# An adaLN transformer block for 32 batches: the set-up of the first batches reordered, and the first batch's stacks loaded in six parts

## The chip, the cores and the metric

The kernel runs on one core of a Trainium2 chip. The core has a matrix engine (TensorE), an engine for elementwise work and reductions (VectorE), one for activation functions (ScalarE), a general one (GpSimd), and a queue engine (SyncE, SP) that here only issues transfers. Each works through its own list of instructions in order and waits on semaphores for the others. The metric is the device time of one execution in microseconds.

## The reference, cut to what matters

```python
# x: (32, 256, 128); 16 heads of 8 channels; feed-forward width 352
mod = (silu(c) @ wmod).reshape(32, 6, 1, 128)
sa, ca, ga, sb, cb, gb = (mod[:, i] for i in range(6))
ga = (2 * (ga >= 0) - 1) * maximum(abs(ga), 0.25)        # gb in the same way
h = layernorm(x) * (1 + ca) + sa
# attention over channels-by-time, heads split along the flattened (t, d) axis
q, k, v = ((h @ W + b).reshape(32, 16, 8, 256) for W, b in ((Wq, bq), (Wk, bk), (Wv, bv)))
attn = softmax(einsum('bhdt,bhds->bhts', k, v) * temperature)
x = x + ga * einsum('bhdt,bhts->bhds', q, attn).reshape(32, 256, 128)
h = layernorm(x) * (1 + cb) + sb
# fp4_linear: both operands rounded blockwise (16) to the FP4 grid
x = x + gb * fp4_linear(silu(fp4_linear(h, w_gate)) * fp4_linear(h, w_up), w_down)
```

## The kernel before

One batch of 256 x 128 values is the unit of work, and 32 of them pass through a software pipeline written out by hand. Each engine has a function `step(k)`, called for k = 0 to 38 and followed by a list of its own for the end of the kernel. In `step(k)` the line `at(k, lag, task)` does `task` for batch `k - lag` if there is such a batch; a line `if k == n: task()` places work that is done once. The order of the lines in `step` is the order of that engine's instructions, so moving a line moves the work in the queue. What is in the queue behind a wait waits too.

A batch goes this way. SP loads x into `x_in` (`load_first_x` for batch 0). VectorE takes the statistics (`stats1_rows`, `variance1`, which also makes the negated mean), GpSimd the reciprocal root (`rstd1_pow`) and the normalised rows (`normalise1`). TensorE transposes them (`x_transpose`), ScalarE copies the result out with shift and scale (`h_out`). TensorE projects keys and values into one bank (`kv_proj`) and queries into another (`q_proj`). The float32 keys and values are split into a high and a low part by four VectorE instructions (`v_hi`, `k_hi`, `v_lo`, `k_lo`), eight DMAs store the parts to an internal DRAM tensor (`store_k_hi` and so on, semaphore `split_stored`), and five DMAs load them back in another arrangement: `v_stack` (512 KB) and four row groups of `k_stack` (128 KB each), all on one semaphore, `stack_loaded`. `k_stack` must be zeroed first, in four pieces per buffer (`zero_k(p, i)` on GpSimd); each of the two buffers is zeroed once.

`scores(b, c, j)` for j = 0 to 15 then makes one head's scores, two matmuls each, in the order `head(j) = j % 4 * 4 + j // 4`; head h needs group h // 4 of `v_stack`, and row group h % 4 of `k_stack`. VectorE takes the row maxima of two heads at a time (`maxes`), ScalarE the exponentials (`exps`), TensorE the product with the queries (`mix`). The second half of the block (gates, second norm, quantised feed-forward) follows some steps later.

Set-up work is placed among the first steps. TensorE's `condition()` multiplies the shift and scale part of the modulation, VectorE's `shift_and_scale()` copies it out; `h_out(0)` needs it. TensorE's `gates()` and VectorE's `gates()` (six instructions) make the other four parts, which SP stores (`store_mod`) and loads per batch (`load_mod`). The feed-forward weights are quantised once, in a chain that goes back and forth between VectorE (`ff_max`, `ff_recip`, `ff_exponent`, `ff_magic`) and GpSimd (`ff_scale`, `ff_y`, `ff_add`, `ff_sub`, `ff_rescale`). The three bias rows and the temperatures come with SP's `load_set_up`; ScalarE's and VectorE's `biases()` split the biases.

In the kernel before, `scores(0, c, 0)` waits for all five loads at once, and `kv_proj(0)` for the biases ahead of its first matmul.

## Time and profile before

| | |
|---|---|
| median of 3 runs | 618.02 us (617.03 to 620.19) |
| the profiled execution: its own time | 614.91 us |
| its span, from the first to the last instruction | 613.1 us |
| mean granted TensorE clock over the span | 0.969 |
| busy: TensorE, VectorE, ScalarE, GpSimd | 555.5, 567.7, 555.8, 507.3 us |

Times in the trace count from the start of the span. "Busy" sums the time in which an engine works on instructions; a wait stands as idle time ahead of an instruction, with the engine or transfer that ended it. An issue of a DMA and the landing of its data are different things: the landing time is counted from the start of the issue. The granted clock is 1.00 where TensorE is granted 2.4 GHz, and 0.50 where it is granted 1.2 GHz.

### The profile page before, as it was taken

To read this page: it belongs to the slowest core of one execution; us is meant where nothing else is said; L and a number is where in the kernel's file an instruction comes from. 1 tells how busy PE (TensorE), PEld (TensorE's weight loads), DVE (VectorE), ACT (ScalarE), POOL (GpSimd) and SP (SyncE) were. 2 spreads that over 40 slices of the span, in tenths; PEclk is the share of its full clock that TensorE was granted. 3 is DMA by queue.
4 is the path that set the end of the run, shared out by engine and by line. 5 is a ranking of instruction groups with operands and counts; after the bars stand their busy time and mean duration, and the time that the engine had idled before them with its cause. 6 is when DMAs were issued, how large, how long until landed. Compare 5 with 4: busy or idle time off the path is not lost.

```text
span 613.1 us, 15512 instructions
## 1 busy us (share of the span) xinstructions
PE 555.5 (91%) x4336; PEld 383.2 (63%) x4336; DVE 567.7 (93%) x1124; ACT 555.8 (91%) x2281; POOL 507.3 (83%) x710
## 2 busy tenths in 40 slices
PE   4478899999999999999999999999999999998865
PEld 2355555666666666666666666666666666666554
DVE  3478799999999999999999999999999999999996
ACT  2199899999999999999999999999999999999721
POOL 7343478899999999999999999999999999998751
PEclk9669799999999999999999999999999999999987
DMA  3746654555555655565455665556555666543000
GB/s 92 199 123 157 163 150 129 156 158 150 148 149 149 170 150 148 153 173 162 136 151 148 164 171 154 155 143 166 144 145 149 158 174 165 151 128 95 10 10 26
DMA packets 87872, 86.12 MB, mean 140 GB/s; under 512 B 8550, under 2 KB 83532, under 8 KB 87788
## 3 DMA queue, kind: packets, MB, share of 16 engines
q1 hardware_dynamic: 85628, 83.37, 50.5%
q10 hardware_dynamic: 2160, 1.77, 1.1%
q8 instruction: 36, 0.59, 0.4%
q14 instruction: 48, 0.39, 0.3%
HBM read 47.29 MB, written 37.81 MB: 139 GB/s over the span
## 4 chain that ended last, share of the span: by engine, by line
ACT 54%; PE 16%; issue 12%; DVE 12%; POOL 2%; DMA 2%; SPq 1%; DVEq 0%; ACTq 0%; POOLq 0%
ACT probs L785 48%; DVE neg_max L961 6%; PE score_ps L1453 5%; PE bank L1531 5%; PE bank L1520 3%; ACT hT L795 2%; DVE silu_g L1079 2%; ACT hid_T L819 2%; ACT q_T L801 1%; DVE h_mag L931 1%; PE bank L1556 1%; DMA k_stack<-split_dram 1%; PE bank L1498 1%; POOL hid_q L345 1%; ACT tanh_g L813 1%
## 5 line engine op out<-in xcount | busy, mean ns | idle before, releaser
L785 ACT ACTIVATE probs<-score_ps,neg_max 128x256 f32<-128x256 f32 x1024 | 483.6, 553 | 5.2 <-DVE neg_max L961 4.2
L961 DVE TENSOR_REDUCE neg_max<-score_ps 128x4 f32<-128x1024 f32 x256 | 312.0, 1219 | 18.5 <-PE score_ps L1453 15.8
L785 ACT ACTIVATION_READ_ACCUMULATOR probs<-score_ps,neg_max 128x1 f32 x1024 | 292.8, 286 | 0.0
L1453 PE MATMUL score_ps<-v_stack,k_stack 128*128 128x256 f32 x1024 | 233.6, 331 | 25.6 <-ACT probs L785 22.7
L1453 PEld LDWEIGHTS score_ps<-v_stack,k_stack 128*128 128x128 f32 x1024 | 154.9, 193 | 109.6 <-ACT probs L785 89.9
L1498 PE MATMUL bank<-probs,q_z 128*32 128x256 f32 x2048 | 131.5, 387 | 0.0
L1498 PEld LDWEIGHTS bank<-probs,q_z 128*32 128x32 f32 x2048 | 57.3, 110 | 41.7 <-issue 2.1
L1556 PEld LDWEIGHTS bank<-wd_T,hid_T 118*128 118x128 f32 x384 | 52.6, 201 | 7.5 <-ACT hid_T L819 1.3
L1556 PE MATMUL bank<-wd_T,hid_T 118*128 118x128 f32 x384 | 55.6, 285 | 0.5 <-ACT hid_T L819 0.5
L1520 PE MATMUL bank<-wgu_T,h_T 128*128 128x352 f32 x128 | 51.5, 484 | 1.7 <-ACT h_T L808 0.5
L345 POOL TENSOR_TENSOR hid_q<-hid_r,hid_sc 128x704 f32<-128x704 bf16 x31 | 43.0, 1386 | 6.4 <-DVE hid_r L340 6.3
L1531 PE MATMUL bank<-wgu_T,h_T 128*128 128x352 f32 x128 | 48.0, 459 | 0.0
L336 POOL TENSOR_TENSOR hid_q<-hid_q,hid_mag 128x704 f32<-128x704 f32 x30 | 45.8, 1527 | 1.8 <-DVE hid_mag L935 1.8
L819 ACT ACTIVATE hid_T<-bank 118x384 f32<-118x384 f32 x64 | 33.3, 523 | 14.2 <-PE bank L1545 14.0
L1473 PE MATMUL bank<-w_kv,hT 128*128 128x256 f32 x128 | 42.0, 422 | 1.4 <-ACT hT L795 1.4
L813 ACT ACTIVATE tanh_g<-bank 128x352 f32<-128x352 f32 x64 | 39.0, 609 | 4.6 <-PE bank L1520 4.5
L340 POOL TENSOR_TENSOR hid_r<-hid_q,hid_mag 128x704 bf16<-128x704 f32 x28 | 42.8, 1530 | 0.0
L318 POOL TENSOR_TENSOR hid_q<-hid,hid_rs 128x704 f32<-128x704 f32 x30 | 41.6, 1388 | 0.6 <-DVE hid_rs L1098 0.2
L516 POOL TENSOR_TENSOR rstd<-var,minus_half 128x2 f32<-128x2 f32 x32 | 22.8, 712 | 20.7 <-DVE var L969 18.2
L530 POOL TENSOR_TENSOR rstd<-var,minus_half 128x2 f32<-128x2 f32 x32 | 30.2, 945 | 11.7 <-DVE nm L972 7.9
L1545 PE MATMUL bank<-ident,hid_q 128*118 128x128 f32 x192 | 28.8, 286 | 10.9 <-POOL hid_q L345 6.5
L268 POOL TENSOR_SCALAR h_c<-x,nm,rstd 128x128 f32<-128x128 f32 x62 | 31.8, 520 | 3.2
(119 smaller groups left out, 877.8 us busy)
## 6 DMA issues: line engine op xcount, KB each, us to landing
v_stack<-split_dram SPq DMA_DIRECT2D x32, 512.0 KB, 4.2
split_dram<-kv_hi SPq DMA_DIRECT2D x124, 128.0 KB, 2.6
split_dram<-kv_lo SPq DMA_DIRECT2D x124, 128.0 KB, 2.7
k_stack<-split_dram SPq DMA_DIRECT2D x124, 128.0 KB, 4.5
mod_bc<-mod_dram SPq DMA_DIRECT2D x32, 256.0 KB, 3.9
x_in<-in_L_attn_x_dram SPq DMA_DIRECT2D x32, 128.0 KB, 3.2
out_dram<-out_t SPq DMA_DIRECT2D x32, 128.0 KB, 3.6
split_dram<-kv_hi ACTq DMA_DIRECT2D x4, 128.0 KB, 2.4
```

The costliest lines, as they stand in the source:

```text
L336: ve.tensor_tensor(hid_q[:, :], hid_q[:, :], hid_mag[:, :], ALU.add).then_inc(hid_t_made, 1)
L340: ve.tensor_tensor(hid_r[:, :], hid_q[:, :], hid_mag[:, :], ALU.subtract)\
L345: ve.tensor_tensor(blocks16(hid_q[:, :]), blocks16(hid_r[:, :]), spread16(hid_sc[:, :]), ALU.mult).then_inc(hid_dq_made, 1)
L785: nc.scalar.activation(probs[p][:, h, a, :], score_ps[:, j % 4, a, :], ACT.Exp, bias=neg_max[:, p, n:n + 1], accum_out=row_sum[:, p, h, a: ...
L813: nc.scalar.activation(tanh_g[:, a, :], bank_gate[a][:, 0:FF], ACT.Tanh, scale=0.5)\
L819: nc.scalar.activation(hid_T[:, a, :, :], bank_hidT[a][0:HN, 0:HT * 128].rearrange("p (t n) -> p t n", n=128), ACT.Copy)\
L961: nc.vector.tensor_reduce(neg_max[:, p, 4 * u:4 * u + 4], score_ps[:, lo:lo + 2, :, :].rearrange("p b a n -> p (b a) n"), AX.X, ALU.max, n ...
L1453: done = nc.tensor.matmul(score_ps[:, j % 4, a, :], k_stack[p][:, h, 128 * a:128 * a + 128], v_stack[p][:, h // R, :], start=True, stop=True)
L1498: done = nc.tensor.matmul(bank_mix[32 * g:32 * g + 32, 0:T], q_z[p][:, a, g, r, :], probs[p][:, R * g + r, a, :], start=(i == 0), stop=(i ...
L1520: nc.tensor.matmul(bank_gate[a][:, 0:FF], h2_T[:, 128 * a:128 * a + 128], wgu_T[:, 0, :], start=True, stop=True).then_inc(gate_ps_made[a], 1)
L1531: nc.tensor.matmul(bank_up[a][:, 0:FF], h2_T[:, 128 * a:128 * a + 128], wgu_T[:, 1, :], start=True, stop=True).then_inc(up_ps_made[a], 1)
L1556: done = nc.tensor.matmul(bank_down[:, a * D:(a + 1) * D], hid_T[:, a, t, :], wd_T[:, t, :], start=(t == 0), stop=(t == HT - 1))
```

## The change

Six things are done. The order of the set-up work on all engines is another: SP issues `w_mod`, then biases and temperatures, and only then the feed-forward weights; `condition()` is TensorE's first step; VectorE takes batch 0's statistics ahead of `shift_and_scale`, `biases` and the weight maxima; GpSimd zeroes only one piece of `k_stack` ahead of batch 0's rstd, three behind its `normalise1`, and the four of the second buffer behind batch 1's. `gates()` goes behind `q_proj(0)` on TensorE and behind `variance1(1)` on VectorE, ahead of `ff_max(0)`. Batch 0's stacks are loaded in six parts, each with a semaphore of its own: four row groups of `k_stack` and two halves of `v_stack`; SP issues k 0, v 0, k 2, and ScalarE v 1, k 1, k 3, ahead of `h_out(1)`. Batch 0's scores wait at j = 0 for v 0 and k 0, at j = 2 for v 1, at j = 4, 8 and 12 for k 1, 2 and 3. `kv_proj(0)` waits for the biases behind its first matmul. Batches from 1 on are loaded as before.

```diff
@@ helpers
+        def wait_stacks(eng, b):
+            if b == 0:
+                for part in (*first_v, *first_k):
+                    eng.wait_ge(part, 16)
+            elif b > 0:
+                eng.wait_ge(stack_loaded[b % 2], (b + 1) // 2 * LOADS * 16)
...
+        def load_first_v(eng, i):
+            wait_dma(eng, split_stored, 0, STORES * 16)
+            groups = slice(i * G // 2, (i + 1) * G // 2)
+            eng.dma_start(v_stack[0][:, groups, :].bitcast(F32),
+                          split_dram[0, 1, groups].rearrange("g r s j n -> (r s j) g n")).then_inc(first_v[i], 16)
+
+        def load_first_k(eng, r):
+            eng.wait_ge(k_zeroed[0], G)
+            wait_dma(eng, split_stored, 0, STORES * 16)
+            eng.dma_start(k_stack[0][32 * r:32 * r + 32, r:H:R, :].bitcast(F32),
+                          split_dram[0, 0, :, r].rearrange("g s j n -> (s j) g n")).then_inc(first_k[r], 16)
@@ SP, step
+                if k == 0:
+                    load_first_x()
+                if k == 0:
+                    load_w_mod()
+                if k == 0:
+                    load_set_up()
                 if k == 2:
                     load_ff(1)
-                if k == 0:
-                    load_first_x()
...
+                if k == 5:
+                    load_first_stacks()
+                if k == 5:
+                    load_first_ks()
                 at(k, 5, load_stacks_first)
-                if k == 3:
-                    load_set_up()
                 at(k, 3, load_x)
                 at(k, 5, store_v_hi)
-                if k == 0:
-                    load_w_mod()
                 if k == 5:
                     store_mod()
@@ GpSimd, step
+                if k == 0:
+                    zero_q()
+                if k == 0:
+                    zero_k(0, 0)
...
                 at(k, 6, normalise1)
+                if k == 7:
+                    ff_y(1)
                 if k == 7:
                     ff_y(2)
...
                 if k == 7:
-                    zero_k(1, 3)
+                    ff_y(0)
                 if k == 6:
-                    zero_k(1, 2)
+                    zero_k(0, 1)
                 if k == 6:
                     zero_k(0, 2)
                 if k == 6:
                     zero_k(0, 3)
+                if k == 6:
+                    ff_scale(2)
+                if k == 6:
+                    ff_scale(1)
                 if k == 7:
+                    zero_k(1, 0)
+                if k == 7:
+                    zero_k(1, 1)
+                if k == 7:
+                    zero_k(1, 2)
+                if k == 7:
+                    zero_k(1, 3)
@@ ScalarE, step
+                if k == 6:
+                    load_first_va()
+                if k == 6:
+                    load_first_ka()
                 at(k, 6, load_k_stack)
...
+                if k == 5:
+                    biases()
                 at(k, 5, h_out)
@@ VectorE, step
-                if k == 7:
-                    gates()
                 at(k, 7, v_hi)
...
-                if k == 4:
-                    shift_and_scale()
...
                 at(k, 6, stats1_rows)
-                if k == 2:
-                    ff_max(2)
...
                 at(k, 6, variance1)
+                if k == 7:
+                    gates()
+                if k == 7:
+                    ff_max(0)
+                if k == 7:
+                    ff_exponent(1)
+                if k == 7:
+                    ff_recip(0)
+                if k == 6:
+                    shift_and_scale()
+                if k == 6:
+                    biases()
+                if k == 6:
+                    ff_max(2)
+                if k == 6:
+                    ff_max(1)
+                if k == 6:
+                    ff_recip(2)
                 if k == 6:
                     ff_recip(1)
@@ TensorE, scores
-                if j == 0:
-                    wait_dma(pe, stack_loaded, b, LOADS * 16)
-                    if b == 0:
+                if b == 0:
+                    if j == 0:
                         pe.wait_ge(modT_made, 2)
                         pe.wait_ge(mod_step, 6)
+                    if j % (G // 2) == 0 and j < G:
+                        pe.wait_ge(first_v[j // (G // 2)], 16)
+                    if j % G == 0:
+                        pe.wait_ge(first_k[j // G], 16)
+                elif j == 0:
+                    wait_stacks(pe, b)
@@ TensorE, kv_proj
-                    pe.wait_ge(bias_step, 3)
-                    pe.wait_ge(pad_zeroed, 2)
                 for a in range(2):
...
+                    if b == 0:
+                        pe.wait_ge(bias_step, 3)
+                        pe.wait_ge(pad_zeroed, 2)
                     done = nc.tensor.matmul(cols, ones_r[:, 0:128], b_pad[:, D:3 * D], start=False, stop=True,
@@ TensorE, step
+                if k == 0:
+                    condition()
...
                 at(k, 7, q_proj)
+                if k == 7:
+                    gates()
...
-                if k == 4:
-                    gates()
-                if k == 3:
-                    condition()
```

## Rows read from the trace of the kernel before

**Rows 1.** Busy time by stretches: stretch, its length, busy us (instructions) of each engine, granted clock, DMA share, GB/s.

```profile
30.00:84.00 54.00, 44.42 (x281) 29.06 (x285) 42.23 (x72) 50.89 (x215) 24.80 (x42) 0.84 0.57 146
84.00:534.00 450.00, 434.50 (x3541) 300.84 (x3541) 443.54 (x865) 449.07 (x1861) 414.93 (x574) 1.00 0.57 154
```

**Rows 2.** The chain of waits, 0 to 60 us: start, us, what.

```profile
9.33 0.73 POOL rstd L516
...
11.15 0.70 PE bank L1461 x2
...
12.54 1.19 PE bank L1473 x2
...
14.80 0.23 PE bank L1476
...
17.80 3.23 DMA split_dram<-kv_lo
...
22.10 5.40 DMA k_stack<-split_dram
```

**Rows 3.** The timeline of TensorE: start, us, instruction, [idle before and what ended it].

```profile
6.55 1.92 PE L1419 MATMUL score_ps<-w_mod,silu_c 128*32 128x512 f32 x2
...
15.30 0.52 PE L1486 MATMUL bank<-ones_r,b_pad 128*128 128x256 f32 x1
...
25.29 0.78 PE L1476 MATMUL bank<-b_pad,ones_r 128*128 128x256 f32 x1
...
27.54 1.88 PE L1453 MATMUL score_ps<-v_stack,k_stack 128*128 128x256 f32 x8 [0.41 <-DMA k_stack<-split_dram]
...
57.30 0.67 PE L1473 MATMUL bank<-w_kv,hT 128*128 128x256 f32 x2
```

**Rows 4.** The timeline of SP's queue: start and us of DMA issues.

```profile
1.18 0.40 SPq L389 DMA_DIRECT2D x_in<-in_L_attn_x_dram  x1
...
2.58 1.38 SPq L413 DMA_DIRECT2D w_ff<-in_L_ffn_w_up_dram  x3
...
5.77 0.61 SPq L405 DMA_DIRECT2D temp<-_L_attn_temperature_dram  x1
```

**Rows 5.** DMA issues, 1.1 to 2.9 us: count, KB each, us to landing.

```profile
x_in<-in_L_attn_x_dram SPq DMA_DIRECT2D x1, 128.0 KB, 2.9
...
w_ff<-in_L_ffn_w_up_dram SPq DMA_DIRECT2D x1, 64.0 KB, 3.3
```

**Rows 6.** The timeline of VectorE.

```profile
7.82 0.42 DVE L977 BATCH_NORM_STATS2 stats<-x_in 128x6 f32<-128x256 f32 x1
...
9.32 0.41 DVE L911 TENSOR_SCALAR mod_rows<-score_ps 32x256 f32<-32x256 f32 x1
...
10.81 0.55 DVE L921 SCALAR_TENSOR_TENSOR mod_rows<-mod_rows,mod_tmp 32x256 f32<-32x256 f32 x1
...
17.10 0.54 DVE L926 TENSOR_REDUCE w_am<-w_ff 128x24 f32<-128x384 f32 x1
```

**Rows 7.** The timeline of GpSimd.

```profile
3.80 1.84 POOL L505 MEMSET k_stack<- 128x1024 f32 x2
...
17.73 0.31 POOL L261 TENSOR_SCALAR w_sc<-w_am 128x24 f32<-128x24 f32 x1 [3.96 <-DVE w_am L926]
...
30.87 0.91 POOL L617 TENSOR_TENSOR w_ff<-w_ff,w_mag 128x384 f32<-128x384 f32 x1 [7.92 <-DVE w_mag L935]
```

**Rows 8.** The timeline of ScalarE.

```profile
6.89 1.07 ACT L750 ACTIVATE b_pad<-b_raw 1x384 fp32r<-1x384 f32 x2 [3.17 <-DMA b_raw<-in_L_attn_bv_dram]
...
30.06 0.47 ACT L785 ACTIVATE probs<-score_ps,neg_max 128x256 f32<-128x256 f32 x1 [0.56 <-DVE neg_max L961]
...
70.88 0.47 ACT L785 ACTIVATE probs<-score_ps,neg_max 128x256 f32<-128x256 f32 x1 [1.59 <-DVE neg_max L961]
```

**Rows 9.** Busy time by stretches, with the columns of the first group.

```profile
43.00:62.50 19.50, 15.18 (x125) 10.09 (x124) 16.59 (x27) 18.56 (x80) 6.86 (x12) 1.00 0.56 143
64.00:69.50 5.50, 5.38 (x32) 2.92 (x32) 2.93 (x7) 5.03 (x21) 3.18 (x7) 0.50 0.56 165
```

More of the change, by code:

```diff
@@ L131, in adaln_block @@
         stack_loaded = [sem(f"stack_loaded{i}") for i in range(2)]
+        first_v, first_k = ([sem(f"first_{n}{i}") for i in range(m)] for n, m in (("v", 2), ("k", R)))
         out_stored = [sem(f"out_stored{i}") for i in range(2)]
@@ L223, in store_k_hi_on @@
         def store_k_hi_on(eng, b, c):
-            wait_dma(eng, stack_loaded, b - 2, LOADS * 16)
+            wait_stacks(eng, b - 2)
             wait_batches(eng, k_hi_made, b + 1)
@@ L228, in store_v_hi_on @@
         def store_v_hi_on(eng, b, c):
-            wait_dma(eng, stack_loaded, b - 2, LOADS * 16)
+            wait_stacks(eng, b - 2)
             wait_batches(eng, v_hi_made, b + 1)
@@ L246, in load_v_stack_on @@
                 .then_inc(stack_loaded[c % 2], 16)
+        def load_first_v(eng, i):
[8 more added lines that the diff above has]
+                          split_dram[0, 0, :, r].rearrange("g s j n -> (s j) g n")).then_inc(first_k[r], 16)
         def load_k_stack_on(eng, b, c, r):
[L249 removed]
+            if b == 1:
                 eng.wait_ge(k_zeroed[b], G)
@@ L439, in store_v_lo, with load_first_stacks, load_first_ks @@
                     store_v_lo_on(sp, b, c)
+            def load_first_stacks():
+                load_first_k(sp, 0)
+                load_first_v(sp, 0)
+            def load_first_ks():
+                load_first_k(sp, 2)
             def load_stacks_first(b, c):
-                if b < 2:
+                if b == 1:
                     load_v_stack_on(sp, b, c)
@@ L637, in step @@
                 at(k, 10, scale2)
-                if k == 3:
-                    zero_k(0, 0)
                 at(k, 10, shift2)
@@ L642, in step @@
                 at(k, 10, h2_scale)
-                if k == 0:
-                    zero_q()
                 if k == 11:
                     ff_sub(2)
-                if k == 7:
-                    ff_y(1)
                 at(k, 9, q_scaled)
@@ L654, in step @@
                 at(k, 12, hid_rescale)
+                if k == 9:
+                    ff_add(2)
+                at(k, 10, h2_sub)
+                at(k, 6, normalise1)
+                if k == 7:
+                    ff_y(1)
                 if k == 7:
                     ff_y(2)
-                if k == 9:
-                    ff_add(2)
-                if k == 1:
-                    zero_k(1, 0)
-                if k == 3:
-                    ff_scale(1)
                 if k == 7:
-                    zero_k(1, 3)
-                at(k, 10, h2_sub)
-                at(k, 6, normalise1)
+                    ff_y(0)
                 if k == 6:
-                    zero_k(1, 2)
+                    zero_k(0, 1)
                 if k == 6:
@@ L672, in step @@
                     zero_k(0, 3)
+                if k == 6:
+                    ff_scale(2)
+                if k == 6:
+                    ff_scale(1)
                 if k == 7:
-                    ff_y(0)
+                    zero_k(1, 0)
[5 more added lines that the diff above has]
+                    zero_k(1, 3)
                 if k == 11:
@@ L679, in step @@
                 at(k, 9, residual1)
-                if k == 1:
-                    zero_k(1, 1)
                 at(k, 10, h2_rescale)
@@ L692, in step @@
                     ff_sub(1)
-                if k == 3:
-                    zero_k(0, 1)
                 at(k, 11, hid_y)
-                if k == 2:
-                    ff_scale(2)
             for k in range(TAIL):
@@ L770, in store_v_lo, with load_first_va, load_first_ka @@
                     store_v_lo_on(act, b, c)
+            def load_first_va():
+                load_first_v(act, 1)
+                load_first_k(act, 1)
+            def load_first_ka():
+                load_first_k(act, 3)
             def load_k_stack(b, c):
-                if b < 2:
+                if b == 1:
                     for r in range(R // 2, R):
@@ L834, in step @@
                 at(k, 7, exps, 0)
-                if k == 4:
-                    biases()
                 at(k, 7, exps, 1)
@@ L1259, in step @@
                 at(k, 6, variance1)
+                if k == 7:
[16 more added lines that the diff above has]
+                    ff_recip(2)
                 if k == 6:
                     ff_recip(1)
-                if k == 6:
-                    biases()
                 at(k, 10, h2_magic)
-                if k == 7:
-                    ff_max(0)
-                if k == 2:
-                    ff_recip(2)
                 at(k, 11, silu, 1)
-                if k == 2:
-                    ff_max(1)
-                if k == 7:
-                    ff_exponent(1)
                 if k == 8:
```

7 lines of the change are left out of this document (removed).

## The prediction

> **What bounds the kernel now.** I read the busy time by stretches first [rows 1]. From 84 to 534 us ScalarE works 449.07 of 450 us: the exponentials of all batches follow one another without a hole, and this stretch can only be moved, not shortened, by a change to the ramp. From 30 to 84 us ScalarE already works 50.89 of 54 us, so 3.11 us of idle time stand there. Ahead of 30.06 us, where the first exponential starts [rows 8], there is none at all. The kernel's ramp is thus what the change can move: the question is when `exps(0, 0)` starts, and whether the 3.11 us behind it grow.
>
> The chain of waits [rows 2] shows what sets 30.06. Batch 0's rstd starts on GpSimd at 9.33, its transpose on TensorE at 11.15, `kv_proj(0)` at 12.54, with its banks full at 14.80 + 0.23 = 15.03. The split stores end at 17.80 + 3.23 = 21.03, and the stack loads at 22.10 + 5.40 = 27.50. Then scores, maxima, exponentials. A second chain of nearly the same length runs beside it: `kv_proj(1)`, `q_proj(1)` stand ahead of `scores(0, 0)` in TensorE's order, and the score row shows TensorE idle only 0.41 us ahead of it [rows 3]. The loads were late by 0.41 us, no more; without them the scores would start at 27.13.
>
> **The change, batch 0.** Before, rstd(0) at 9.33 stood behind weight scales and memsets on GpSimd. `x_in(0)` was issued at 1.18 and took 2.9 us, so it lay there at 4.1 [rows 4, 5]; the statistics take 0.42 us on VectorE [rows 6] and the reduction behind them about 0.2 by my estimate, hence 4.8. After the change GpSimd has only `zero_q` and one `zero_k` ahead; two of these start at 3.80 and take 1.84 us, 0.92 each [rows 7], so GpSimd is free at 4.72. From rstd to the start of the transpose the chain took 11.15 − 9.33 = 1.82, so the transpose can start at 4.8 + 1.82 = 6.6. TensorE must do `condition()` first; that ended where `gates()` began, at 6.55, held by `w_mod` [rows 3], which keeps its place in SP's order. I take 6.65 for the transpose. Transpose to full banks took 15.03 − 11.15 = 3.88, hence 10.53: batch 0 comes **4.50 us** earlier.
>
> Three things stand beside this. The set-up DMAs (three bias rows and the temperatures) took 5.77 + 0.61 − 3.96 = 2.42 us to issue, 0.6 each [rows 4]; they now begin two issues of 0.46 behind 1.18, at 2.1, so the third bias row goes out at 3.3. With the 2.9 us of `x_in` to landing it is there at 6.2, with the 3.3 of `w_up` at 6.6 [rows 5]; ScalarE's two copies take 1.07 us [rows 8] and stand ahead of `h_out(0)`, whose transpose ends at 7.35. So they end at 7.3 or 7.7: I take 0, and 0.4 late as the bound. `w_down` and `w_up` move back by those 2.4 us: `w_up`, last issued at 3.5 and now at 5.9, with 3.3 us to landing is there at about 9, its maximum ends at 9.5, and GpSimd scales it behind three `zero_k` that end at 6.6 + 2.8 = 9.4. VectorE's reciprocals, which now stand ahead of `v_hi(0)`, end near 10.5, just as the banks fill: 0 by my sum, 0.5 late as the bound. The wait for the biases moves behind the first projection matmul: that gives up to that matmul's 0.6 us if they are late, and nothing where they are in time.
>
> **The change, batch 1.** Before, its banks were full at 25.29 + 0.78 = 26.07, which is 11.04 after those of batch 0 [rows 3]. Now `gates()` stands ahead of its transpose on TensorE, and on VectorE ahead of `ff_max(0)`, whose scale on GpSimd stands ahead of rstd(1). Counted from batch 0's full banks: `q_proj(0)` ends at 15.30 + 0.52 − 15.03 = 0.79; `gates()` takes 1.92 (two matmuls), to 2.71; its six VectorE steps took 11.36 − 9.32 = 2.04, to 4.75 [rows 6]; `ff_max(0)` and the hand-over took 17.73 − 17.10 = 0.63, to 5.4; the scale 0.31 [rows 7] with a hand-over of the same size as the others, under 0.1, to 5.79; rstd to transpose 1.82 and transpose to full banks 3.88, to 11.5. That is **0.45 us worse** than 11.04: `gates()` costs 2.71 + 2.04 here, and what was there before in its place, two scalings `ff_y` and one memset between rstd's neighbours, has moved behind `normalise1(1)`. Bounds: with TensorE at its upper level `gates()` would take half, and the chain would gain up to 0.65.
>
> ScalarE passes three load issues ahead of `h_out(1)` and waits for the stores first. The stores landed 21.03 − 15.03 = 6.0 after the banks [rows 2]; two issues took 22.10 − 21.03 = 1.07, so three bring it to 7.6, and the transpose of batch 1 ends at 11.5 − 3.88 + 0.7 = 8.3: covered by 0.7. On SP, `store_mod` and `load_mod(0)` keep their places behind the loads, and the gates are ready at 4.75, ahead of them; batch 0 needs them only behind its mix, which follows all its exponentials.
>
> **The parts.** The loads took 27.5 − 21.03 = 6.47 from the stores' landing to the last landing. Undivided they would land at 6.0 + 6.5 = 12.5 after the banks; the scores can start at 11.5 + 1.06 (27.13 − 26.07) = 12.56. So the 0.41 us wait goes even without the parts, and waiting for them singly gives 0 to 0.4. The shorter first part could save more only if TensorE had nothing ahead of the scores, and it has `kv_proj(1)`.
>
> Behind the scores nothing of the order is new: 27.54 to 30.06 is 2.52 us, and ScalarE sat idle 0.56 us ahead of its first exponential [rows 8], so its own queue (the stores of `kv_lo(1)`, `q_T`) has that much slack, of which the missing 0.41 us wait uses most. The four `zero_k(1, ·)` move behind `normalise1(1)`: 3.7 us on GpSimd, which then stood idle for 7.92 us before `ff_add(1)` [rows 7]; with the 0.8 us scalings ahead they end 5 us before batch 1's stores have landed, which the loads wait for as well.
>
> **Sum:** 4.50 − 0.45 + 0.41 = 4.46, say 4.5 us. First exponentials at 25.6. ScalarE is full behind them, so all is carried to the end. The profiled execution took 614.91 us (span 613.1 and 1.8 around it), which would become 610.4. It lies 3.1 below the shown median of 618.02; the shift against the median gives **613.5**.
>
> **Rivals.** 0.5% of this kernel is 3.1 us, about what a measurement can tell from no change.
>
> A, the sum as above: 613.5, own range 612 to 615. Chance 0.48.
>
> B, half of it lost in new waits: biases late 0.4, reciprocals ahead of `v_hi(0)` 0.5, and one more TensorE stall of the kind that left ScalarE idle 1.59 us at 70.88 [rows 8]. That stall stands in a stretch where the granted clock was 0.50 (1.2 GHz) and TensorE worked 5.38 of 5.5 us [rows 9]. One such stall alone: 4.5 − 1.6 = 2.9, 615.1; with the 0.5 ahead of `v_hi(0)`: 615.6. For it: the margins in the ramp are tenths of a microsecond. Chance 0.24.
>
> C, nothing gained: the ramp is shorter but batch 1's part, stores of `kv_lo(1)`, loads, four more memsets, holds ScalarE's queue at `load_k_stack(1)`. It needs those to slip by 4.5; the memsets have 5 us of slack, the stores move with the banks. 618. Chance 0.07.
>
> D, more than the sum: `kv_proj(1)` at the upper level. Two of its matmuls take 1.19 us in the ramp and 0.67 once the granted clock is 1.00 in the stretch around them [rows 2, 3, 9], so it would end 1.1 earlier, and `gates()` gives 0.65: 6.2, 611.8. If the 3.11 us of idle time [rows 1] vanish too, 608.7. TensorE is now busy without a hole from `kv_proj(0)` through `gates()`, which speaks for it; a hole of 6 us follows, which speaks against. Chance 0.15.
> The Trainium skill (TensorE: Matmul & The Clock Gate, Part 1) says that the point at which the clock rises varies from run to run of the same kernel. By that rule `kv_proj(1)` and `gates()` can come out on either level in different runs, and a median over runs lies between A and D. The changes of level in this trace agree in so far as they follow neither batch nor stage; one trace can't show the variation.
>
> E, slower: the upper level's stretch is lost. From 43 to 62.5 us TensorE worked 15.18 of 19.5 us at 1.00 [rows 9]. At half that clock the same work takes 30.4 us, 10.9 more than there is; less the 4.5, the kernel is 6.4 slower, 624.4. Each microsecond at the lower level costs 0.56, so 7.6 us of loss, which makes it slower by over 0.5%, needs 13.6 us of that stretch. Against it: after 64 to 69.5, with TensorE full, the level rose again. Chance 0.06.
>
> **Numbers.** Faster by over 0.5% in A and D: 0.63; within in B and C: 0.31; slower 0.06. The range leaves out the lower part of D, half of C and all of E: 610.0 to 618.5.
>
> **What would show it.** In the profile after: rstd(0) at 4.8, `kv_proj(0)`'s banks full near 10.5, `gates()` right behind `q_proj(0)`, rstd(1) near 16.3, `kv_proj(1)`'s banks near 22, first scores near 23.1 with no wait for a load ahead of them, first exponentials near 25.6, ScalarE idle 3 us in the 54 us behind. Wrong if a DMA ends the wait ahead of the scores, if `gated` or the stores hold VectorE, or if the idle time behind the first exponentials is over 5 us.

## The result, and the profile after

| | before | changed |
|---|---|---|
| median on the same chip | 617.52 us (6 runs, 616.79 to 620.46) | 613.49 us (6 runs, 611.20 to 614.23) |
| ratio | | 0.9931, 95% interval 0.9913 to 0.9949 |
| profiled execution: own time, span | 614.91, 613.1 us | 614.23, 611.3 us |

The changed kernel is 4.0 us faster in the medians, 0.7%. Its profiled span is only 1.8 us shorter. That difference is explained below; the span of one execution is not the effect.

The timeline of TensorE after, which answers to [rows 3]:

```profile
5.32 1.04 PE L1458 MATMUL score_ps<-silu_c,w_mod 128*128 128x32 f32 x4 [2.44 <-DMA w_mod<-in_L_wmod_dram]
6.48 0.69 PE L1510 MATMUL bank<-ident,xn 128*128 128x128 f32 x2
7.87 1.19 PE L1520 MATMUL bank<-w_kv,hT 128*128 128x256 f32 x2 [0.70 <-ACT hT L835]
...
9.57 0.78 PE L1526 MATMUL bank<-b_pad,ones_r 128*128 128x256 f32 x1
...
11.34 1.42 PE L1463 MATMUL score_ps<-w_mod,silu_c 128*32 128x512 f32 x2
17.39 0.69 PE L1510 MATMUL bank<-ident,xn 128*128 128x128 f32 x2 [4.63 <-POOL xn L556]
18.78 1.19 PE L1520 MATMUL bank<-w_kv,hT 128*128 128x256 f32 x2 [0.70 <-ACT hT L835]
...
20.47 0.78 PE L1526 MATMUL bank<-b_pad,ones_r 128*128 128x256 f32 x1
...
22.11 1.22 PE L1502 MATMUL score_ps<-v_stack,k_stack 128*128 128x256 f32 x8
25.75 3.44 PE L1502 MATMUL score_ps<-v_stack,k_stack 128*128 128x256 f32 x8 [2.41 <-ACT probs L825]
```

The reader is to see three things. Batch 0's banks are full at 9.57 + 0.78 = 10.35, where [rows 2] had 15.03. Then comes a hole of 4.63 us ahead of batch 1's transpose, ended by GpSimd. And the first score row, at 22.11, has no wait ahead of it at all; the one in [rows 3] waited 0.41 us for a load.

The granted clock that the profile gives is 1.00 over these first microseconds, but that is no reading. The first entry in the trace's list of clock changes is a rise, at 12.1 us here and at 15.4 in the profile of before, and ahead of the first entry the profile gives 1.00. The durations up to there are those of the lower level (the pair at 7.87 took 1.19 us).

The timelines of GpSimd, of ScalarE and of VectorE after:

```profile
4.72 0.72 POOL L549 TENSOR_TENSOR rstd<-var,minus_half 128x2 f32<-128x2 f32 x1
...
15.24 0.30 POOL L283 TENSOR_SCALAR w_sc<-w_am 128x24 f32<-128x24 f32 x1 [5.36 <-DVE w_am L970]
15.62 0.72 POOL L549 TENSOR_TENSOR rstd<-var,minus_half 128x2 f32<-128x2 f32 x1
```

```profile
16.03 0.43 ACTq L261 DMA_DIRECT2D v_stack<-split_dram  x1
16.55 0.91 ACTq L267 DMA_DIRECT2D k_stack<-split_dram  x2
18.11 0.56 ACT L835 ACTIVATE hT<-bank,mod_T 128x256 f32<-128x256 f32 x1 [4.27 <-PE bank L1510]
...
24.31 0.38 ACT L841 ACTIVATE q_T<-bank 128x256 f32<-128x256 f32 x1 [5.63 <-issue]
24.59 0.47 ACT L825 ACTIVATE probs<-score_ps,neg_max 128x256 f32<-128x256 f32 x1
```

```profile
22.90 1.23 DVE L1005 TENSOR_REDUCE neg_max<-score_ps 128x4 f32<-128x1024 f32 x1
```

GpSimd is held 5.36 us by VectorE's maximum of the gate weights, which stands behind `gates()`; that is the wait that the change put ahead of batch 1's rstd. The first exponential follows `q_T` without a hole, and the maxima that it needs were done at 22.90 + 1.23 = 24.13, 0.46 us earlier: it is now ScalarE's own queue (four issues of stores for batch 1, then `q_T`) that holds it, not the maxima as in [rows 8]. From batch 1's full banks to the first exponential it is 24.59 − 21.25 = 3.34 us.

**Where the time went after that.** All exponentials run on ScalarE in order, so the execution can be cut at the start of the first exponential of batches 0, 3 and 31 (the 1st, 97th and 993rd of 1024 in ScalarE's timeline). I did this for every profile of this study. "Low" is how long the granted clock was 0.50 between the first two cuts, from stretches of half a microsecond.

| kernel | first exponential | to batch 3 | low in it | batch 3 to 31 | from there to the end of the span |
|---|---|---|---|---|---|
| before | 30.06 | 51.23 | 17 | 480.45 | 51.4 |
| before, second profile (`b_again`) | 29.77 | 51.11 | 17 | 480.47 | 54.5 |
| changed | 24.59 | 53.02 | 23.5 | 480.48 | 53.2 |
| changed, second (`a_again`) | 25.07 | 52.01 | 20.5 | 480.49 | 53.0 |
| changed, third (`a_again2`) | 24.49 | 52.91 | 23.5 | 480.43 | 53.3 |
| `b_parts` | 29.29 | 51.97 | 20.5 | 480.49 | 53.1 |
| `a_whole` | 25.85 | 51.93 | 20.5 | 480.46 | 53.1 |
| `a_gates_old` | 26.03 | 52.85 | 24 | 480.47 | 53.3 |
| `a_gates_late` | 24.47 | 50.78 | 17 | 480.52 | 53.0 |
| `a_gates_hout` | 23.61 | 51.83 | 20.5 | 480.47 | 53.3 |
| `a_gates_hout_whole` | 25.33 | 51.94 | 23.5 | 480.45 | 51.3 |
| `a_fill` | 24.60 | 50.21 | 10 | 480.52 | 53.0 |
| `a_fill_mid` | 24.28 | 51.03 | 13.5 | 480.51 | 53.1 |
| `a_best` | 24.13 | 50.80 | 12 | 481.41 | 53.4 |

The gain at the first exponential was 5.5 us in the first pair of profiles. 1.8 of it was lost before batch 3, nothing in the 480 us behind, and 1.8 in the last part, where the first profile of before was lucky: the same kernel took 51.4 and 54.5 there. The clock goes with that too: in this last part it was at 0.50 for 10.6 us in the two profiles that took 51.3 to 51.4, for 13.7 to 15.6 in the ten that took 53.0 to 53.3, and for 17.2 in the one that took 54.5; `a_best` (10.2 us low, 53.4) is the exception. Over the profiles of the two kernels (two of before, three of the changed one), the change gains 5.2 us at the first exponential, loses 1.5 up to batch 3 and about 0.3 in the last part, in the mean.

The busy time by stretches of the changed kernel, with TensorE alone (stretch, its length, busy us, granted clock, DMA share, GB/s):

```profile
26.00:39.00 13.00, 11.67 (x35) 0.50 0.46 131
39.50:42.50 3.00, 1.85 (x12) 1.00 0.59 156
43.00:46.00 3.00, 3.00 (x19) 0.50 0.73 183
47.00:59.00 12.00, 9.71 (x77) 1.00 0.51 132
60.50:66.00 5.50, 5.39 (x40) 0.50 0.55 153
```

Against [rows 9], where the clock was 1.00 from 43 to 62.5 without a break, there is a further stretch at 0.50 near 43 to 46, when the first `mix` runs (from 44.7).

### The profile page after: what moved, and what is told of

Read it like the earlier page. It is cut to its first block, busy times and chain, and to the rows that moved or that the text cites. A ratio compares the mean times of both kernels' runs of the same rounds, so it can differ in the third digit from the quotient of the medians.

```text
span 611.3 us, 15522 instructions
## 1 busy us (share of the span) xinstructions
PE 558.3 (91%) x4336; PEld 385.6 (63%) x4336; DVE 568.7 (93%) x1124; ACT 555.9 (91%) x2281; POOL 507.3 (83%) x710
## 4 chain that ended last, share of the span: by engine, by line
ACT 52%; PE 18%; issue 13%; DVE 12%; POOL 3%; ACTq 1%; DVEq 0%; POOLq 0%
ACT probs L825 47%; DVE neg_max L1005 6%; PE score_ps L1502 6%; PE bank L1581 5%; PE bank L1570 3%; ACT hT L835 2%; DVE silu_g L1123 2%; ACT hid_T L859 2%; PE bank L1548 2%; PE bank L1606 1%; ACT q_T L841 1%; DVE h_mag L975 1%; POOL hid_q L367 1%; PE bank L1520 1%; DVE h_mag L979 1%
## 5 line engine op out<-in xcount | busy, mean ns | idle before, releaser
L1502 PE MATMUL score_ps<-v_stack,k_stack 128*128 128x256 f32 x1024 | 234.9, 333 | 24.2 <-ACT probs L825 21.7
L859 ACT ACTIVATE hid_T<-bank 118x384 f32<-118x384 f32 x64 | 33.3, 523 | 13.7 <-PE bank L1595 13.5
L1595 PE MATMUL bank<-ident,hid_q 128*118 128x128 f32 x192 | 28.5, 284 | 12.2 <-POOL hid_q L367 6.3
```

Source lines behind the costliest of these rows:

```text
L859: nc.scalar.activation(hid_T[:, a, :, :], bank_hidT[a][0:HN, 0:HT * 128].rearrange("p (t n) -> p t n", n=128), ACT.Copy)\
L1502: done = nc.tensor.matmul(score_ps[:, j % 4, a, :], k_stack[p][:, h, 128 * a:128 * a + 128], v_stack[p][:, h // R, :], start=True, stop=True)
```

## The experiments

Each kernel was timed beside the kernel before, in four groups, each on one chip: `a_again`, `a_whole`, `b_parts` and `a_gates_old`; `a_gates_late`, the two `a_gates_hout` and `a_fill`; `a_again2`, `a_fill_mid` and `a_best`; `b_again`. Apart from the kernel before (two profiles) and the changed one (three), each has one profile, so what is said of times within it rests on one execution. The first pair, above, is a group of its own.

**1. The changed kernel again (`a_again`), and once more (`a_again2`).** No edit.

> The changed kernel unchanged, for its spread and for a second profile. Theory S (the sum of the ramp): the first exponential starts at 24.6 us again, give or take 0.2, since everything ahead of it is set by instructions of fixed length. Theory C (the clock ate part of the gain): in the first profile the batches' exponentials started 5.5 us earlier at batch 0 but 3.7 us earlier from batch 3 on; if the TensorE clock's low stretches did that, the second profile shows low stretches at other places and another shift from batch 3 on, anywhere from 2.5 to 6. Rival (the order of work behind the ramp did it): the loss between batch 0 and batch 3 is again 1.8, to within 0.2. Time about 613.5.

> The changed kernel once more, on the chip of the two below, as their measure, and as a fourth profile of its clock. Both theories: ratio to the kernel before 0.991 to 0.993; from the first exponential to the start of batch 3's it takes 52 to 53 us, as in the two profiles so far.

Measured: 612.18 us, ratio 0.9915 (0.9894 to 0.9936), and 613.00 us, ratio 0.9924 (0.9896 to 0.9953). Three measurements of the same change thus give 0.9915 to 0.9931. The first exponential came at 25.07 and 24.49. The 0.6 us between them has one place: `gates()` took 1.92 us on TensorE in the one and 1.29 in the other, and everything behind it moves along. The timeline of TensorE of `a_again`:

```profile
11.34 1.92 PE L1463 MATMUL score_ps<-w_mod,silu_c 128*32 128x512 f32 x2
17.88 0.69 PE L1510 MATMUL bank<-ident,xn 128*128 128x128 f32 x2 [4.63 <-POOL xn L556]
```

The wait behind is 4.63 in all three profiles, and the transpose starts at 17.88 against 17.39 and 17.26. So theory S missed with 24.6 give or take 0.2: an instruction ahead of the first exponential is not of fixed length when the clock changes under it. The loss up to batch 3 was 0.8 instead of the rival's 1.8, with 3 us less at the low level. So theory C's variation exists, but the loss was not erratic: each of the three profiles shows 52.0 to 53.0, above the 51.1 and 51.2 of the kernel before. My range of 2.5 to 6 for the shift held (4.2 and 3.9), but it was too wide to be much of a test.

**2. The parts undone (`a_whole`).**

```diff
-                load_first_k(sp, 0)
-                load_first_v(sp, 0)
+                load_v_stack_on(sp, 0, 0)
+                load_k_stack_on(sp, 0, 0, 0)
...
-                    if j % (G // 2) == 0 and j < G:
-                        pe.wait_ge(first_v[j // (G // 2)], 16)
-                    if j % G == 0:
-                        pe.wait_ge(first_k[j // G], 16)
+                        wait_stacks(pe, 0)
```

> The changed order, but batch 0's stacks loaded as before: five DMAs on one semaphore, all awaited at the first score. Theory S: the scores stand behind the second batch's projections, so the loads (issued from 16.1, all landed by about 22.5) are late by at most 0.4 us, and ScalarE's own queue hides most of it: first exponential at 24.6 to 24.9, time within 0.3 us of the changed kernel. Rival P (the parts carry the gain): first exponential 1.5 us or more later, time 1.5 to 4 us longer.

Measured: 611.59 us, ratio 0.9917 (0.9897 to 0.9937), against `a_again`'s 0.9915 on the same chip. The timeline of TensorE shows why nothing is lost:

```profile
5.99 1.04 PE L1453 MATMUL score_ps<-silu_c,w_mod 128*128 128x32 f32 x4 [3.23 <-DMA w_mod<-in_L_wmod_dram]
7.25 0.69 PE L1502 MATMUL bank<-ident,xn 128*128 128x128 f32 x2 [0.22 <-POOL xn L552]
...
23.37 1.49 PE L1494 MATMUL score_ps<-v_stack,k_stack 128*128 128x256 f32 x8
```

The scores follow the projections without a wait, though all five loads were awaited at once. The first exponential was 0.78 later than in `a_again` (I expected at most 0.3 later), but by the rows that is the 0.77 by which the first transpose came late (7.25 against 6.48), waiting for GpSimd; the arrival of the first transfers varies, as `w_mod`'s does here. ScalarE's queue hides a late load as well: the first exponential came 3.34 us behind batch 1's full banks, as with the parts. The rival P falls: in this kernel the parts carry nothing.

**3. The parts alone (`b_parts`).** The order of before, the six loads and single waits of the change.

> The kernel before with the six parts and their single waits alone, order untouched. Theory S: only the 0.41 us wait ahead of the first score can go; first exponential at 29.6 to 30.06, time 0 to 0.4 us shorter than before. Rival P: first exponential 1.5 us or more earlier, time 2 to 4 us shorter than before.

Measured: 615.72 us, ratio 0.9986 (0.9971 to 1.0001), that is −0.9 us with an interval from −1.8 to +0.1. The timeline of TensorE:

```profile
26.24 0.78 PE L1520 MATMUL bank<-ones_r,b_pad 128*128 128x256 f32 x1
26.81 1.48 PE L1487 MATMUL score_ps<-v_stack,k_stack 128*128 128x256 f32 x8
```

The 0.41 us wait of [rows 3] is gone. The first exponential came at 29.29, 0.5 to 0.8 earlier than in the two profiles of before and outside the 29.6 to 30.06 expected. Against the first profile, 0.12 of the 0.77 is batch 1, whose banks were full that much earlier. The rest stands behind the banks: from them to the first exponential it was 3.99 us there (3.88 in `b_again`), with ScalarE waiting for maxima, and 3.34 here, with no such wait, exactly as in the changed kernel. The wait for the load had thus cost 0.5 to 0.65 us there, more than the 0.41 and 0.30 that TensorE stood idle; ScalarE's own queue sets the limit to what removing it can give. The rival's 2 to 4 us are excluded.

**4. Both `gates()` back in their old places (`a_gates_old`).** `gates()` in TensorE's step 4 and ahead of `v_hi(0)` on VectorE.

> The changed kernel with both gates() back where they stood: on TensorE ahead of batch 0's transpose, on VectorE ahead of v_hi(0). Theory S: batch 0's transpose comes 1.8 later (8.3), its banks are full at 12.1; batch 1 no longer waits for gates on VectorE, but ScalarE issues the loads only when the stores have landed, at 17.8, so h_out(1) goes at 19.3 instead of 18.1: first exponential at 25.8, 1.2 us later than in the changed kernel, time 1.2 longer. By the prediction's narrower view, in which the gates on VectorE cost batch 1 2.7 us and nothing else holds it, the first exponential would come no later than 24.6.

Measured: 611.58 us, ratio 0.9931 (0.9906 to 0.9956), which doesn't part it from `a_again`. The trace does: first exponential at 26.03 instead of 24.5 to 25.1, and the wait stands where it was expected, ahead of `h_out(1)` on ScalarE, which had been issuing loads:

```profile
19.54 0.56 ACT L835 ACTIVATE hT<-bank,mod_T 128x256 f32<-128x256 f32 x1 [3.87 <-issue]
```

Moving `gates()` behind the projections is worth 1.0 to 1.5 us at the first exponential, as batch 0's transpose no longer stands behind it. The narrower view, in which it could only cost, falls. But the 1.2 us of time that were expected did not show: the median is 0.6 below `a_again`'s. The single executions tell why. Three had a mean granted clock of 0.962 to 0.966 and took 613.1 to 615.5 us, four had 0.977 and took 610.6 to 611.6: one and the same kernel differs by more than the edit is worth, and the clock goes with it. All eighteen executions of the changed kernel have 0.962 to 0.969.

**5. VectorE's `gates()` behind `ff_max(0)` (`a_gates_late`).**

```diff
                 at(k, 6, variance1)
-                if k == 7:
-                    gates()
                 if k == 7:
                     ff_max(0)
+                if k == 7:
+                    gates()
```

> The changed kernel with VectorE's gates() behind ff_max(0) instead of ahead of it, so that batch 1's rstd on GpSimd no longer waits for the gates. Theory S: rstd(1) starts at 13.6 instead of 15.6 and the transpose of batch 1 ends at 16.0; but h_out(1) on ScalarE stands behind three load issues that wait for the stores (landed at 16.0, issued to 17.5), so of the 2 us only 0.6 reach kv_proj(1): first exponential at 24.0 to 24.4, time 0.6 us shorter than the changed kernel. Rival (the gates' wait alone held batch 1): first exponential 2 us earlier, at 22.6.

Measured: 612.88 us, ratio 0.9941 (0.9923 to 0.9959). Batch 1's rstd started at 13.44 instead of 15.62. ScalarE and TensorE:

```profile
16.38 0.42 ACTq L261 DMA_DIRECT2D v_stack<-split_dram  x1
16.90 0.91 ACTq L267 DMA_DIRECT2D k_stack<-split_dram  x2
17.93 0.56 ACT L835 ACTIVATE hT<-bank,mod_T 128x256 f32<-128x256 f32 x1 [4.10 <-issue]
```

```profile
15.44 0.69 PE L1510 MATMUL bank<-ident,xn 128*128 128x128 f32 x2 [3.01 <-POOL xn L556]
18.60 1.19 PE L1520 MATMUL bank<-w_kv,hT 128*128 128x256 f32 x2 [2.47 <-ACT hT L835]
...
22.45 1.19 PE L1502 MATMUL score_ps<-v_stack,k_stack 128*128 128x256 f32 x8 [0.45 <-DMA v_stack<-split_dram]
```

Of 2.2 us won at rstd, 0.2 reached `h_out(1)`: the transpose is done at 16.1, and ScalarE is still issuing loads until 17.8. The wait moved, and a second one (0.45 for `v_stack`) came up behind it. The first exponential at 24.47 is no earlier than in the best profile of the changed kernel. The expectation's mechanism was right, but its 0.6 us of gain was not seen, and the first exponential missed its 24.0 to 24.4.

**6. And ScalarE's three issues behind `h_out(1)` (`a_gates_hout`); the same with whole loads (`a_gates_hout_whole`).**

```diff
-                if k == 6:
-                    load_first_va()
-                if k == 6:
-                    load_first_ka()
                 at(k, 6, load_k_stack)
...
                 at(k, 5, h_out)
+                if k == 6:
+                    load_first_va()
+                if k == 6:
+                    load_first_ka()
```

> As a_gates_late, and ScalarE's three load issues behind h_out(1) instead of ahead of it. Theory S: h_out(1) goes at 16.1, kv_proj(1)'s banks are full at 19.3 instead of 21.25, the scores are then ready to start at 20.1, and only now do the loads come last: with the parts the first ones have landed at about 20.9. First exponential at 22.6 to 23.2, time 1.5 to 2 us shorter than the changed kernel. Rival (the parts never matter, the loads land together at 22.3): first exponential at 24.2 or later.

> As a_gates_hout, with batch 0's stacks loaded whole and awaited at once, as before the change. Theory S: the scores wait for the last load at 22.3 to 22.6, first exponential at 24.2 to 24.6: 1.5 us later than with the parts, which were worth nothing in the changed kernel. Rival (all transfers share the same engines and land together): no later than with the parts, to within 0.3.

Measured: 611.14 us, 0.9916 (0.9898 to 0.9934), and 612.12 us, 0.9934 (0.9915 to 0.9952), on the same chip. TensorE with the parts, then without:

```profile
18.82 0.78 PE L1536 MATMUL bank<-ones_r,b_pad 128*128 128x256 f32 x1
21.60 1.19 PE L1502 MATMUL score_ps<-v_stack,k_stack 128*128 128x256 f32 x8 [2.00 <-DMA v_stack<-split_dram]
```

```profile
19.59 0.78 PE L1528 MATMUL bank<-ones_r,b_pad 128*128 128x256 f32 x1
22.84 2.05 PE L1494 MATMUL score_ps<-v_stack,k_stack 128*128 128x256 f32 x8 [2.47 <-DMA k_stack<-split_dram]
```

Now the loads come last, and the parts count: scores start at 21.60 with them and at 22.84 without, the first exponential at 23.61 and 25.33. Both are later than the 22.6 to 23.2 and 24.2 to 24.6 expected. Of the 1.7 us between them, 1.2 is the loads; the rest is that the first row of scores took 1.19 us with the parts and 2.05 without, where the granted clock was 0.50. The parts count for less than they could, because of which part is late. The issues of the version with parts:

```profile
v_stack<-split_dram ACTq DMA_DIRECT2D x1, 256.0 KB, 3.6
k_stack<-split_dram SPq DMA_DIRECT2D x2, 128.0 KB, 4.0
v_stack<-split_dram SPq DMA_DIRECT2D x1, 256.0 KB, 4.9
```

The half that the first score needs is SP's, issued second in its queue at 16.43, and takes 4.9 us; ScalarE's half, needed two heads later, was issued at 15.97 and takes 3.6. Another order of the two was not tried. In time the two intervals overlap; that the parts give 1.0 us there is the trace's word and the medians' direction, not a settled ratio.

**7. TensorE kept busy (`a_fill`, `a_fill_mid`).** The second leaves out the 16 ahead of `x_transpose`.

```diff
+            def fill(n):
+                for _ in range(n):
+                    nc.tensor.matmul(bank_3[:, 0:T], b_pad[:, 0:D], ones_r[:, :], start=True, stop=True)
             def scores(b, c, j):
                 p, h = c % 2, head(j)
+                if 4 <= b * H + j < 20:
+                    fill(10 if b * H + j == 4 else 1)
...
+                if k == 7:
+                    fill(16)
                 at(k, 6, x_transpose)
```

> The changed kernel with matmuls of no use (biases by ones, into a bank not used yet) on TensorE: 16 ahead of batch 1's transpose, 10 ahead of the fifth head's scores of batch 0, and one ahead of each of the next 15 heads' scores. Theory C (the low stretches of the clock follow TensorE's idle time in the ramp, and cost the ramp): kv_proj(1) at the upper level (a pair in 0.67 instead of 1.19), first exponential 1.0 us earlier (23.6 to 24.1), no long low stretch between 26 and 40, and the waits of ScalarE for maxima between 28 and 40 (0.33, 0.32, 0.86 us) gone: batch 3 starts 2 to 2.5 us earlier after the ramp than in the changed kernel, time 1.5 to 2.5 shorter. Rival (the clock is no matter in the ramp, ScalarE hides it): first exponential and batch 3 within 0.4 of the changed kernel, or later by what the added matmuls take (up to 1).

> As a_fill, without the 16 matmuls ahead of batch 1's transpose; only the 10 ahead of batch 0's fifth head and the single ones behind. Theory C: the 16 gave nothing, as the clock had fallen again before kv_proj(1); what a_fill won lies behind the first exponential. First exponential at 24.6 to 25.1, batch 3 starts 50.2 to 50.8 later, time as a_fill's 609.3 to within 0.6, and 2 to 3 us below the changed kernel on the same chip. Rival (a_fill's lower time was the chip or chance): same as the changed kernel to within 0.5.

Measured: 609.25 us, ratio 0.9880 (0.9859 to 0.9900), with `a_gates_hout`'s 0.9916 on the same chip; and 610.58 us, ratio 0.9891 (0.9867 to 0.9914), with `a_again2`'s 0.9924 beside it. These are the lowest ratios of the study, but the step from the changed kernel to them is not settled: the intervals of `a_fill_mid` and `a_again2` overlap, and `a_fill` has no changed kernel on its chip. TensorE by stretches in `a_fill`:

```profile
25.00:31.00 6.00, 4.21 (x23) 1.00 0.53 150
32.00:38.00 6.00, 5.96 (x23) 0.50 0.42 105
```

Where the changed kernel had 0.50 from 26 to 39, this one holds 1.00 to 31, and the two waits of 0.33 and 0.32 us for maxima at 28.7 and 32.7 are gone (the third, 0.86 at 39.6, is 0.67, with a new one of 0.33 behind it); batch 3 comes 50.2 us behind the first exponential. The 16 matmuls gave nothing: the clock had fallen again at 17.6, ahead of `kv_proj(1)`, whose pair took 1.19 still. So half of what I expected of `a_fill` failed (kv_proj at the upper level, first exponential 1.0 earlier), and the gain behind it came (50.2 to batch 3 against 52.0 to 53.0). In `a_fill_mid` the first exponential came at 24.28 (24.6 to 25.1 expected) and the stretch up to batch 3 took 51.0, longer than the 50.2 to 50.8 expected; the gain over the changed kernel was 2.4 us in the medians. What speaks for it beyond one profile is the clock of all timed executions: the mean granted clock was 0.972 to 0.980 in each of the 16 of `a_fill`, `a_fill_mid` and `a_best`, and 0.962 to 0.969 in each of the 18 of the changed kernel.

**8. All together (`a_best`).** The edits of 5 and 6 with parts, `fill(12)` ahead of the transpose, `fill(8)` ahead of the first score, the rest as in `a_fill_mid`.

> All that helped: gates() on VectorE behind ff_max(0), ScalarE's three loads behind h_out(1), the parts kept, 12 matmuls of no use ahead of batch 1's transpose, 8 ahead of the first score (which waits 2 us for v_stack there), and the fill behind it as in a_fill_mid. Theory S and C add up: first exponential at 23.2 to 23.7, batch 3 starts 50.2 to 50.8 later, at 73.5 to 74.5; time 1 us below a_fill_mid, 3 to 4 us below the changed kernel. Rival (the two gains overlap: an earlier start only meets later stalls): no shorter than a_fill_mid.

Measured: 611.33 us, ratio 0.9894 (0.9871 to 0.9917): no shorter than `a_fill_mid`. The rival holds. TensorE:

```profile
16.61 0.67 PE L1528 MATMUL bank<-w_kv,hT 128*128 128x256 f32 x2 [0.70 <-ACT hT L835]
...
18.34 1.12 PE L1489 MATMUL bank<-ones_r,b_pad 128*128 128x256 f32 x8
22.07 1.61 PE L1510 MATMUL score_ps<-v_stack,k_stack 128*128 128x256 f32 x8 [2.61 <-DMA v_stack<-split_dram]
23.48 2.33 PE L1489 MATMUL bank<-ones_r,b_pad 128*128 128x256 f32 x10
```

`kv_proj(1)` finally ran at the upper level (0.67 for the pair), and the 1.1 us that this gave went into a longer wait for `v_stack`, which is issued when batch 0's stores have landed. The first exponential, at 24.13, missed the 23.2 to 23.7 expected. Behind it the clock had fallen, so ten matmuls of no use took 2.33 us instead of 1.35. The 480 us part was 0.9 longer in this one profile. The excess is spread evenly, about 0.03 us in each batch (17.21 instead of 17.18), so it is not a stall that the edits made; its cause stays open.

**9. The kernel before again (`b_again`).**

> The kernel before, unchanged, for a second profile. In its first profile the time fell into 30.06 us to the first exponential, 51.23 from there to batch 3's, 480.45 from batch 3's to batch 31's, and 51.36 from batch 31's to the end of the span; the changed kernel's three profiles show 53.0, 52.0 and 52.9 in the second part and 53.2, 53.0 and 53.3 in the last. Theory C (the first profile of before fell on favourable places of the clock, and its own time of 614.9 lies under its median of 617.5 for that reason): the second profile shows 30.1 +- 0.3, 51.5 to 53, 480.5, and 53.0 to 53.3: a span near 615.5. Rival (the changed kernel itself costs 1 to 2 us behind the ramp): again 51.2 and 51.4, a span near 613.

Measured: 617.39 us, ratio 1.0020 (1.0002 to 1.0037) to itself. Two measurements of one and the same kernel on one chip thus differed by 0.2%, outside their interval; a difference of 0.2% between two kernels here means nothing. The profile answered both ways: the last part was 54.5 instead of 51.4, so the first profile had been lucky there (theory C, which had expected 53.0 to 53.3), but the part from the first exponential to batch 3 was again 51.1 (the rival).

## Why the prediction came out as it did

Predicted 613.5 (610.0 to 618.5), measured 613.49. In what was really forecast, the shift, it was 4.5 against 4.0 us: the prediction set out from the 618.02 of three runs, and the kernel before came to 617.52 over six. Point by point:

- **Batch 0**: banks full at 10.53 predicted, 10.35 in three profiles. The chain from rstd to the full banks moved as a block (rstd started at 4.72 instead of 9.33), which no run here undid by itself; the biases (copied from 5.63 to 6.70) and `v_hi(0)` (10.38, 0.16 behind the reciprocals) were covered as argued.
- **Batch 1**: 11.5 behind batch 0 predicted, 10.90 in the first profile, 11.40 in `a_again`, 10.78 in `a_again2`. The term was right at the lower level; the bound of 0.65 for `gates()` at the upper level was what the first and the third mostly drew. What I sized wrongly is the whole move: it was booked as a cost of 0.45 against before, but `a_gates_old` shows that the alternative, `gates()` ahead of batch 0's transpose, costs 1.0 to 1.5 more.
- **The loads**: no wait ahead of the scores, with parts or without (`a_whole`). In the kernel before, the wait was sized at the 0.41 us that TensorE stood idle; `b_parts` gave 0.5 to 0.8 at the first exponential.
- **First exponential**: 25.6 predicted, 24.5 to 25.1 measured. The prediction followed the scores: banks full at 22.0, scores 1.06 behind them, the exponential 2.52 behind those, 3.58 in all. The scores did start 0.2 earlier (0.86 behind the banks), but they no longer set the time. ScalarE's queue does, 3.33 to 3.37 behind the banks in all three profiles. So of the 1.0 us in the first profile 0.2 is batch 0, 0.6 batch 1 and 0.2 this last part.
- **"ScalarE is full behind them, so all is carried to the end"**: this is the step that failed in size. From batch 3 on it held to 0.1 us over 480 us in all but one profile. Between the first exponential and batch 3 the changed kernel took 52.0 to 53.0 against 51.1 to 51.2, a loss of 0.8 to 1.9. The ScalarE idle time from 30 to 84 us rose from 3.11 to 4.32; over the same work, in the 54 us from the first exponential, it rose from 3.05 to 4.62, where "What would show it" had about 3:

```profile
30.00:84.00 54.00, 47.75 (x317) 30.88 (x317) 41.58 (x71) 49.68 (x208) 26.21 (x45) 0.82 0.53 142
24.59:78.59 54.00, 45.65 (x270) 29.79 (x271) 40.03 (x67) 49.38 (x208) 23.73 (x40) 0.78 0.53 142
```

The two errors cancel: 0.5 to 1.1 us more at the start, 0.8 to 1.9 less behind. The agreement to 0.01 us is luck, and the start from a median 0.5 above the later one is part of it. That the ramp's chain of waits would move the whole kernel by about 4 us is not luck.

**What ate it** is the clock, which was rivals B and E of the prediction, with another price. Over the fourteen profiles the part up to batch 3 follows the time at the low level: 10 us low goes with 50.2, 17 with 50.8 to 51.2, 20.5 with 51.8 to 52.0, 23.5 to 24 with 51.9 to 53.0 (12 and 13.5 lie between). From end to end that is about 0.2 us per microsecond at 0.50 ((52.9 − 50.2) / (23.5 − 10)), against the 0.56 that rival E took. A likely reason is that for part of a low stretch ScalarE, not TensorE, is the slower: from 26 to 39 us TensorE worked 11.67 of 13 us, not all of it. The 0.2 mixes kernels with one profile each. Among the 140 timed executions, compared within one kernel and one chip, a further microsecond at 0.50 anywhere in the span goes with about 0.1 us; so 0.1 to 0.2 is what the record supports. `a_fill` shows that this is a cause and not only a companion: with nothing changed but matmuls whose result nobody reads, low time and stalls fell together, and the total with them as far as the intervals tell. The changed kernel has the more low time because its scores now start in a burst that is over at 23.3 and followed by a hole of 2.41 us, after which the clock was 0.50 for 13 us. In `a_fill_mid`, where ten matmuls fill that hole down to 1.21 us, the level held until 28.5. Why the kernel before has the same 17 us in both its profiles while `b_parts`, 0.5 to 0.8 us earlier, has 20.5, stays open: no run here varied the place of a hole alone.

The Trainium skill (TensorE: Matmul & The Clock Gate, Part 1) says that the point of the rise varies from run to run of one kernel. The three profiles of the changed kernel agree: `gates()`, at the same 11.34, took 1.42, 1.92 and 1.29 us, and the first rise in the trace's list stands at 12.1, 13.2 and 11.9 us.

Rival A gave the number. In its parts it was A with two others mixed in: B's new stalls in a low stretch (1.6 us more ScalarE idle time) and D's faster `gates()` (0.5 to 0.6 us in two of three profiles). The versions with the lowest times are `a_fill` and `a_fill_mid`, 1.1 to 1.2% below before; `a_fill_mid` is 2.4 us below the changed kernel in the medians, with intervals that overlap.

## What to carry to other kernels

In a ramp several chains of nearly equal length run side by side, and an edit is worth the distance to the second longest: the six parts were worth nothing in the changed kernel, and 1.2 us at the first score once two other waits had been taken away. Every gain was eaten by the next wait in line (GpSimd's rstd, then ScalarE's issues, then `v_stack`; in the changed kernel ScalarE's queue stood 0.46 us behind the maxima), so read what stands 0.5 us behind the wait that you remove.

Cut the trace at points that all versions pass, such as the first exponential of batches 0, 3 and 31. A total that differs by 0.2% between two measurements of one kernel can't place a gain of 1 us, but such a table can. And look at the mean granted clock of every timed execution: in `a_gates_old` it split one kernel into two groups 3 to 4 us apart.

If one engine waits for another in short holes, its clock is part of the path. Twenty-five matmuls of no use, in holes that were there anyway (`a_fill_mid`), gave 2.4 us in the medians, against 4.0 for the whole reordering; the intervals overlap, and the higher granted clock in every one of their executions is the firmer sign.

## What the runs showed of the hardware that I had not expected

- The same 256 KB transfer landed in 3.6 us from ScalarE's queue and in 4.9 from SP's, issued within 0.5 us of each other, SP's behind a 128 KB transfer in its queue (`a_gates_hout`). The nine other profiles with these six loads show 3.5 to 3.9 and 4.9 to 5.4.
- The fill matmuls (128x256) took 0.135 us each at the upper level (16 in 2.16) and up to 0.23 in `a_best`; ten of them ahead of a score took 1.35 us in `a_fill_mid` and 2.33 in `a_best`, once the clock had fallen.
- The trace's list of clock changes begins with a rise (12.1, 13.2 and 11.9 us in the changed kernel, 15.4 and 28.6 in the kernel before); ahead of it the profile gives 1.00, while a pair of matmuls takes 1.19 us there as at 0.50, against 0.67 at 1.00.
- The last part of the same program, from batch 31's first exponential, took 51.4 us in one profile of before and 54.5 in another: 0.5% of the kernel, more than most edits here.
